# Latent keys and values of all batches made in the prologue, from chunk means that PE makes beside the transposes

## The chip, the cores and the metric

The kernel runs on one core of a Trainium2 chip. The metric is the device time of one execution in microseconds; of the kernel before there are three timed runs and one profiled execution. TensorE is called PE, VectorE DVE, ScalarE ACT, GpSimd POOL and SyncE SP, as in the profile; PEld is PE's loading of weights.

## What is computed

The input x has 4 batches of 1024 tokens with 256 features. It is normalised over the features to xn, and the output is x + attention(xn) + experts(xn).

- Attention is local, with 16 heads of 16 features over the last 128 tokens, and remote: the tokens of a batch are averaged in 64 chunks of 16 (`pooled`), `rkv = pooled @ rkv_w + rkv_b` gives latent keys and values (4 heads of 16 features each), and each token attends to the chunks before its own. A gate mixes both parts, and an output projection follows.
- The experts: a router picks 8 of 64 experts for each token, and their weighted outputs are added, with one shared expert for all tokens.

What matters here is that the latent keys and values of a batch depend on all its chunk means, while a block of 128 tokens uses only chunks that end before its tokens do. A batch has 8 blocks, and each block holds 8 chunks.

## The kernel before, in words

The 4096 tokens are 32 blocks (`NB`) of 128. Each engine has its own instruction stream, written out by hand, and semaphores tie them together.

**Prologue.** SP loads x in four parts, then the weights. DVE measures and normalises the blocks (`normalise`, L1204) into a ring of eight places (`xn_st`): a place is free again when PE has turned its block and SP has stored it to DRAM (L363, `xn_tiles`). PE goes through pairs of blocks (L660): `turn_x` transposes a pair into one of four PSUM banks (`turn_banks`, L648), and `route` of the pair before multiplies the transposed blocks with the router's weights (L656). ACT copies the transposed pair to `xT_all` (L935) and makes the router's scores (L939). Behind its last store SP fills the expert slots in DRAM with zeros (L368), 80 DMAs from the tile `zeros`, which is the second half of the experts' weight buffers. DVE then works out the routing: top groups (L1257 to L1279), top 8 (L1282, L1285), the selection (L1287), ranks with PE's help (L671, L673, then L1292 to L1301), slots (L1307 to L1335). POOL builds constants (L442 to L487), changes weights (L489 to L506), and adds the output bias to x (L513). When slots are known and the zeros have landed, it begins to scatter token rows to the experts' slots with indirect DMAs (L557). The order on PE is: turns and logits, rank products, attention.

**Attention** runs blocks 0 to 15 ahead of the experts and 16 to 31 behind them (`attention(start)`), the first two and the last of each half written out, 13 as a loop. A block's body has 8 steps `s`, one for each pair of heads, the same on PE, ACT and DVE. PE makes the scores of pair s (L741), turns the probabilities of pair s-2 (L755) and multiplies those of pair s-3 with the values (L767 to L769). DVE masks the scores and finds the maximum (L1457), ACT takes the exponential (L1033) and copies the turned probabilities (L1041). Projections of the next block, the shared expert and the remote part are spread over the steps. For the remote part of block i:

- ACT stages the transposed block in `xTs` (L976), DVE sums its 16-token chunks into `pooledT` and copies them a second time (`pool_chunks`, L1348 and L1350, at step 5 for the block after).
- PE's `latent_kv` (L771, step 3) waits for `pooled` and `remote_kept` and makes keys and values of the whole batch so far (L776, L778) in the bank `psM`; they count for chunks up to this block, and the mask `lat_wide` hides the rest.
- DVE's `keep_rkv` (step 3) adds the biases: L1407 spreads the keys over four heads (`rkz`), L1411 the values (`rv`).
- PE's `latent_scores` (L785, step 4), DVE's `latent_max` (L1421 to L1426, step 5), ACT's exponential (L1047), PE's turn and product (L791, L797, step 7), DVE's `latent_out`, and PE's projection one block later.

ACT's `keep_v_mid` (L988) copies the block's values for the windows that straddle two blocks; PE waits for it ahead of the values of pair 0 (step 3, L762). In the first half POOL scatters rows during attention, in the second it gathers the experts' rows (L609) and DVE adds them to x (L1506, twice a step). POOL's DMAs are paced by PE's steps (`pace`).

## Time and profile before

| | |
|---|---|
| timed runs | 1619.88, 1622.6, 1625.2 us; median 1622.6 |
| the profiled execution's own time | 1624.25 us |
| its span, first to last instruction | 1622.7 us |
| PE | 1340.4 us busy, 83% |
| weight loads on PE | 1235.2 us, 76% |
| DVE | 924.8 us, 57% |
| ACT | 905.3 us, 56% |
| POOL | 702.7 us, 43% |
| mean granted clock of PE | 0.91 |

Busy times are shares of the span. The shares are means over stretches that differ: prologue (to 131 us), first attention half, experts, second attention half. A float32 product of PE is two records in the trace, each with its own weight load; a transpose is one. Ends of matmuls are modelled. In a row the text in square brackets is the idle time of the engine before the instruction, and what ended it. "issue" stands for time without a wait that the profile shows.

### The profile page before, as it was taken

To read this page: it belongs to the slowest core of one execution; us is meant where nothing else is said; L and a number is where in the kernel's file an instruction comes from. 1 tells how busy PE (TensorE), PEld (TensorE's weight loads), DVE (VectorE), ACT (ScalarE), POOL (GpSimd) and SP (SyncE) were. 2 spreads that over 40 slices of the span, in tenths; PEclk is the share of its full clock that TensorE was granted. 3 is DMA by queue.
4 is the path that set the end of the run, shared out by engine and by line. 5 is a ranking of instruction groups with operands and counts; after the bars stand their busy time and mean duration, and the time that the engine had idled before them with its cause. 6 is when DMAs were issued, how large, how long until landed. Compare 5 with 4: busy or idle time off the path is not lost.

```text
span 1622.7 us, 38926 instructions
## 1 busy us (share of the span) xinstructions
PE 1340.4 (83%) x9257; PEld 1235.2 (76%) x9259; DVE 924.8 (57%) x3565; ACT 905.3 (56%) x2362; POOL 702.7 (43%) x841
## 2 busy tenths in 40 slices
PE   5117588788889889999999999999888888878885
PEld 4116478787788778988989898888777877778774
DVE  7986245555454553444444444434467777777775
ACT  2104355555555566666666666665545555555553
POOL 6601656656665621222222222100665656656550
PEclk9658689999898899999999999999898999989987
DMA  7999322222222215777777667654232223222220
GB/s 232 367 405 355 135 85 87 87 87 89 86 89 85 90 54 157 214 217 223 217 212 220 210 210 219 192 160 136 82 92 83 79 76 88 82 83 83 76 81 30
DMA packets 159339, 237.63 MB, mean 146 GB/s; under 512 B 21825, under 2 KB 127042, under 8 KB 159298
## 3 DMA queue, kind: packets, MB, share of 16 engines
q1 hardware_dynamic: 126658, 147.97, 27.4%
q0 software_dynamic: 32640, 89.17, 17.6%
q8 instruction: 18, 0.29, 0.1%
q14 instruction: 23, 0.19, 0.0%
HBM read 111.24 MB, written 125.83 MB: 146 GB/s over the span
## 4 chain that ended last, share of the span: by engine, by line
PE 66%; DVE 12%; issue 8%; another core or an unknown queue 7%; ACT 4%; SPq 1%; DVEq 1%; ACTq 0%; DMA 0%
PE psS L878 18%; PE psS L741 9%; PE psT L862 5%; PE psO L887 4%; PE psM L887 4%; PE psT L755 4%; PE psT L769 2%; PE psV L728 2%; PE psQ L688 2%; PE psV L699 2%; PE psQ L709 2%; DVE x_all L1506 1%; PE psO L767 1%; PE psO L769 1%
## 5 line engine op out<-in xcount | busy, mean ns | idle before, releaser
L609 POOL DMA_INDIRECT shared_mem<-slot_outs,idx_st x256 | 266.4, 1041 | 180.5 <-issue 64.0
L557 POOL DMA_INDIRECT slot_rows<-x_out_st,idx_st x256 | 257.7, 1007 | 165.0 <-issue 66.6
L878 PEld LDWEIGHTS psS<-sm,wt 128*128 128x128 f32 x2560 | 297.8, 191 | 40.4 <-ACT sm L1127 37.1
L878 PE MATMUL psS<-sm,wt 128*128 128x128 f32 x2560 | 323.9, 280 | 3.3 <-ACT sm L1127 1.9
L741 PE MATMUL psS<-kT,qz 128*128 128x192 f32 x1024 | 246.7, 368 | 29.6 <-DVE qz L1389 26.4
L1041 ACT COPY prT<-psT 128x384 f32<-128x384 f32 x256 | 122.0, 477 | 263.7 <-PE psT L755 135.3
L1142 ACT COPY wt<-shared_mem 128x512 f32 x320 | 197.8, 619 | 100.7 <-issue 98.4
L1033 ACT ACTIVATE pr<-sm,nmax 128x192 f32<-128x192 f32 x512 | 205.0, 449 | 59.9 <-DVE nmax L1457 47.9
L741 PEld LDWEIGHTS psS<-kT,qz 128*128 128x128 f32 x1024 | 182.4, 210 | 35.8 <-DVE qz L1389 26.9
L1457 DVE CUSTOM_DVE_ANT_0 sm<-psS,pr 128x192 f32<-128x192 f32 x512 | 162.3, 354 | 49.9 <-issue 48.2
L525 POOL DMA_DIRECT2D shared_mem<-in_L_ffn_We_gate x56 | 39.4, 704 | 334.2 <-PE psM L887 181.6
L1534 DVE TENSOR_TENSOR prT<-psS,prT 128x256 f32<-128x256 f32 x160 | 67.9, 425 | 201.1 <-ACT prT L1133 201.1
L755 PE MATMUL psT<-ident,pr 128*128 128x128 f32 x768 | 138.6, 293 | 30.6 <-ACT prT L1041 21.1
L755 PEld LDWEIGHTS psT<-ident,pr 128*128 128x128 f32 x768 | 106.6, 153 | 44.5 <-issue 36.2
L1506 DVE SCALAR_TENSOR_TENSOR x_all<-shared_mem,w,x_all (+1 forms) x256 | 123.5, 483 | 1.1
L1455 DVE MEMSET met<- 1x1 f32 x256 | 15.1, 59 | 179.4 <-PE psS L741 121.4
L1127 ACT COPY sm<-psT 128x512 f32<-128x512 f32 x160 | 93.6, 585 | 14.9 <-PE psT L862 8.5
L862 PE MATMUL psT<-ident,pr 128*128 128x128 f32 x640 | 96.5, 273 | 4.0 <-issue 3.1
L518 POOL COPY idx_st<-slot_idx 128x8 uint32 (+1 forms) x64 | 15.1, 238 | 188.3 <-DMA slot_outs<-sm 104.7
L1133 ACT ACTIVATE prT<-psS 128x256 f32<-128x256 f32 x160 | 61.3, 383 | 53.5 <-PE psS L878 48.5
L887 PE MATMUL psO<-shared_mem,prT 128*128 x320 | 82.5, 380 | 0.2 <-DVE prT L1534 0.2
L767 PE MATMUL psO<-v_mid,prT 128*128 128x72 f32 x256 | 49.5, 277 | 39.8 <-ACT v_mid L988 28.0
(255 smaller groups left out, 2630.1 us busy)
## 6 DMA issues: line engine op xcount, KB each, us to landing
slot_rows<-wt SPq DMA_DIRECT2D x80, 512.0 KB, 5.2
pr<-slot_rows SPq DMA_DIRECT2D x160, 256.0 KB, 3.1
slot_outs<-sm SPq DMA_DIRECT2D x160, 256.0 KB, 2.4
shared_mem<-in_L_ffn_We_gate POOLq DMA_DIRECT2D x56, 128.0 KB, 3.7
shared_mem<-in_L_ffn_We_up POOLq DMA_DIRECT2D x56, 128.0 KB, 3.9
shared_mem<-in_L_ffn_We_down POOLq DMA_DIRECT2D x56, 128.0 KB, 3.8
x_all<-in_L_attn_x SPq DMA_DIRECT2D x4, 1024.0 KB, 9.5
xn_tiles<-sm SPq DMA_DIRECT2D x32, 128.0 KB, 1.8
```

What stands on the lines that cost most here:

```text
L557: pool.indirect_dma_start(slot_rows, bass.IndirectOffsetOnAxis(ap=idx_st[:, j, k:k + 1], axis=0), x_out_st[:, j % 2, :], None).then_inc(sc ...
L609: pool.indirect_dma_start(rows_in[:, j, k, :], None, slot_outs, bass.IndirectOffsetOnAxis(ap=idx_st[:, j, k:k + 1], axis=0)).then_inc(rows ...
L741: last = mm(psS[:, p % 2, u * WIN:(u + 1) * WIN], qz[:, c, u, heads, :].rearrange("p h t -> p (h t)"), kT[:, c, u * UQ:u * UQ + WIN], star ...
L755: last = nc.tensor.transpose(psT[:, 0, a * P:(a + 1) * P], flat[:, a * P:(a + 1) * P], ident[:])
L862: last = nc.tensor.transpose(psT[:, j % 2, (a * DC + c) * P:(a * DC + c + 1) * P], xs[:, j, a, c * P:(c + 1) * P], ident[:])
L878: last = mm(psS[:, j % 2, (2 * a + n) * P:(2 * a + n + 1) * P], wt[j % 2][:, a, c, n * F:(n + 1) * F], xsT[:, j % 2, a, c, :], start=(c == ...
L887: last = mm((psM, psO)[j % 2][:, a * D:(a + 1) * D], hT[:, j % 2, a, :], ring_d[:, e % RING, :], start=True, stop=True)
L1033: nc.scalar.activation(pr[:, p % 4, par, :], sm[:, p % 4, par, :], ACT.Exp, bias=nmax[:, p % 4, par:par + 1], scale=-1.0).then_inc(probs, 1)
L1041: nc.scalar.copy(prT[:, p % 2].rearrange("p a t -> p (a t)"), psT[:, 0, 0:3 * P]).then_inc(prT_ready, 1)
L1142: last = nc.scalar.copy(wt[j % 2][:, a, :, :], ring_gu[:, e % RING, :, :])
L1457: v.tensor_tensor_reduce(sm[:, p % 4, u, :], psS[:, p % 2, u * WIN:(u + 1) * WIN], mask[:, u * WIN:(u + 1) * WIN], -1.0, -FLOOR, ALU.add, ...
L1506: ins = v.scalar_tensor_tensor(x_all[:, t, :], row, w8[:, t, k:k + 1], x_all[:, t, :], ALU.mult, ALU.add)
```

## The change

Latent keys and values are made once, in the prologue, for all four batches.

- POOL builds `chunk_of`, 128x8, with 1/16 where a token belongs to a chunk. In `turn_x` each transpose of PE is followed by a product with the same tile as weights and `chunk_of` as moving operand, which leaves the chunk means of the block in `psO`. The turns have three banks for it instead of four.
- ACT copies `psO` twice into `pooledT` behind the last scores; `pooledT` now lies in the first half of the experts' weight buffers. PE makes the keys of all batches (2 products of 256 columns) and the values (8 of 64 columns) in `psM`. ACT scales and biases the keys into `rkz`, in four instructions; DVE adds the biases of the values, in two, behind its top-8. PE's rank products wait for these.
- POOL prepares the key bias (`brkz`), and `consts` is raised behind it, after the weights have come.
- In attention `pool_chunks`, `latent_kv` and `keep_rkv` are gone, with their semaphores. `latent_scores` and `latent_values` pick their batch with `i // BPS`. `latent_scores` takes over the wait for `remote_kept`.
- Some tiles (`lsm`, `lneg`, `local`, `mixed`) move into `small`, for room. SP's order is as it was: the zero fill stands behind the last store of a normalised block.

The core of the diff:

```diff
-        pooledT = sb("pooledT", [P, DC, 2, NLAT])
-        rkz = sb("rkz", [P, LH, NLAT])
-        rv = sb("rv", [P, LH, LHD + 1])
+        chunk_of = sb("chunk_of", [P, LPB])
+        brkz = sb("brkz", [P, LH])
+        rkz = sb("rkz", [P, LH, B, NLAT])
+        rv = sb("rv", [P, B, LH, LHD + 1])
...
+        pooledT = wt[0][:].rearrange("p a c n -> p (a c n)").rearrange("p (c b a n) -> p c b a n", c=DC, b=B, a=2)
...
-        turn_banks = (psT[:, 0, :], psT[:, 1, :], psM[:], psO[:])
+        turn_banks = (psT[:, 0, :], psT[:, 1, :], psM[:])
...
+            after(nc.gpsimd.memset(chunk_of[:], 1.0 / CH))
+            fill(chunk_of[:], 0.0, [([[-CH, LPB]], 0, 1, ALU.is_ge), ([[CH, LPB]], CH - 1, -1, ALU.is_ge)])
+            pool.sem_inc(chunk_ready, 1)
...
-            nc.gpsimd.memset(pooledT[:], 0.0).then_inc(consts, 1)
             pool.wait_ge(w_in, W_ALL)
-            nc.gpsimd.tensor_scalar(brk[:], brk[:], float(CH), None, ALU.mult).then_inc(brk_ready, 1)
+            nc.gpsimd.tensor_tensor(brkz[:], rk_head[:], brk[:].broadcast_to([P, LH]), ALU.mult).then_inc(consts, 1)
...
-                if m >= 4:
-                    pe.wait_ge(xT_kept, m - 3)
+                if m >= 3:
+                    pe.wait_ge(xT_kept, m - 2)
                 for n in range(2):
                     for c in range(DC):
-                        last = nc.tensor.transpose(turn_banks[m % 4][:, (n * DC + c) * P:(n * DC + c + 1) * P],
-                                                   xn_st[:, (2 * m + n) % XN, c * P:(c + 1) * P], ident[:])
+                        part = xn_st[:, (2 * m + n) % XN, c * P:(c + 1) * P]
+                        nc.tensor.transpose(turn_banks[m % 3][:, (n * DC + c) * P:(n * DC + c + 1) * P], part, ident[:])
+                        at = c * B * NLAT + (2 * m + n) * LPB
+                        last = mm(psO[:, at:at + LPB], part, chunk_of[:], start=True, stop=True)
                 last.then_inc(xn_turned, 1)
...
+            pe.wait_ge(pooled, DC)
+            for c in range(DC):
+                mm(psM[:, 0:B * NLAT], wrkv[:, c, :], pooledT[:, c, :, 0, :], start=(c == 0), stop=(c == DC - 1))
+            for b in range(B):
+                at = B * NLAT + b * LD
+                for c in range(DC):
+                    last = mm(psM[:, at:at + LD], pooledT[:, c, b, :, :].rearrange("p a n -> p (a n)"), wrkv[:, c, LD:2 * LD],
+                              start=(c == 0), stop=(c == DC - 1))
+            last.then_inc(lat_kv, 1)
+            pe.wait_ge(rk_kept, LH + 2)
...
+            def batch(i):
+                return bass.ds(i // BPS, 1)
...
-            def latent_kv(i, nth):
-                pe.wait_ge(pooled, i + 1)
+            def latent_scores(i, nth):
+                pe.wait_ge(rq_kept, i + 1)
                 if nth:
                     pe.wait_ge(remote_kept, i)
-                for c in range(DC):
-                    mm(psM[:, 0:NLAT], wrkv[:, c, :], pooledT[:, c, 0, :], start=(c == 0), stop=(c == DC - 1))
-                for c in range(DC):
-                    last = mm(psM[:, NLAT:NLAT + LD], pooledT[:, c, :, :].rearrange("p a n -> p (a n)"), wrkv[:, c, LD:2 * LD],
-                              start=(c == 0), stop=(c == DC - 1))
-                last.then_inc(lat_kv, 1)
-
-            def latent_scores(i):
-                pe.wait_ge(rk_kept, 3 * i + 3)
-                pe.wait_ge(rq_kept, i + 1)
-                mm(psM[:, 0:LH * NLAT], rqT[:], rkz[:].rearrange("p h n -> p (h n)"), start=True, stop=True).then_inc(lat_s, 1)
+                mm(psM[:, 0:LH * NLAT], rqT[:], rkz[:, :, batch(i), :].rearrange("p h b n -> p h (b n)"), start=True, stop=True).then_inc(lat_s, 1)
...
-                              rv[:, 2 * n:2 * n + 2, :].rearrange("p h d -> p (h d)"), start=True, stop=True)
+                              rv[:, batch(i), 2 * n:2 * n + 2, :].rearrange("p b h d -> p (b h d)"), start=True, stop=True)
...
-                    if s == 3 and live:
-                        latent_kv(i, nth)
...
+            for a in range(2):
+                nc.scalar.copy(pooledT[:, :, :, a, :], psO[:].rearrange("p (c b n) -> p c b n", c=DC, b=B)).then_inc(pooled, 1)
+            act.wait_ge(lat_kv, 1)
+            act.wait_ge(consts, 1)
+            for h in range(LH):
+                nc.scalar.activation(rkz[:, h, :, :].rearrange("p b n -> p (b n)"), psM[:, 0:B * NLAT], ACT.Identity,
+                                     bias=brkz[:, h:h + 1], scale=rk_head[:, h:h + 1]).then_inc(rk_kept, 1)
...
-                    act.wait_ge(pooled, i)
...
+            dve.wait_ge(rk_kept, LH)
+            for par in range(2):
+                r = slice(par * NLAT, (par + 1) * NLAT)
+                tt(rv[r, :, par::2, 0:LHD],
+                   psM[r, B * NLAT:2 * B * NLAT].rearrange("p (b h d) -> p b h d", b=B, h=LH)[:, :, par::2, :],
+                   bcast(brv[r, :].rearrange("p (h d) -> p h d", h=LH)[:, par::2, :], B, 1), ALU.add).then_inc(rk_kept, 1)
...
-            def pool_chunks(i, blk, nth):
-                if nth:
-                    dve.wait_ge(lat_kv, i)
-                dve.wait_ge(xT_staged, i + 1)
-                src = xTs[:].rearrange("p c (n t) -> p c n t", t=CH)
-                v.tensor_reduce(pooledT[:, :, 0, bass.ds(blk * LPB, LPB)], src, AX_X, ALU.add).then_inc(pool_sums, 1)
-                dve.wait_ge(pool_sums, i + 1)
-                v.tensor_copy(pooledT[:, :, 1, :], pooledT[:, :, 0, :]).then_inc(pooled, 1)
...
-            def keep_rkv(i):
-                dve.wait_ge(lat_kv, i + 1)
-                v.scalar_tensor_tensor(rkz[:], bcast(psM[:, 0:NLAT], LH, 1), brk[:], bcast(rk_head[:], NLAT, 2),
-                                       ALU.add, ALU.mult).then_inc(rk_kept, 1)
-                for par in range(2):
-                    r = slice(par * NLAT, (par + 1) * NLAT)
-                    v.scalar_tensor_tensor(rv[r, par::2, 0:LHD],
-                                           psM[r, NLAT:NLAT + LD].rearrange("p (h d) -> p h d", h=LH)[:, par::2, :], 1.0 / CH,
-                                           brv[r, :].rearrange("p (h d) -> p h d", h=LH)[:, par::2, :],
-                                           ALU.mult, ALU.add).then_inc(rk_kept, 1)
...
-                        keep_rkv(i)
...
-                            pool_chunks(i + 1, next_blk, 1)
```

## Rows read from the trace of the kernel before

**Rows 1.** Busy time in stretches; columns: us, engines busy (records), PE clock, DMA share, GB/s.
```profile
22.00:32.00 10.00, 10.00 (x50) 9.96 (x49) 9.86 (x29) 2.54 (x5) 5.85 (x12) 1.00 0.65 218
33.00:48.00 15.00, 14.87 (x129) 14.07 (x129) 14.82 (x30) 8.79 (x15) 14.16 (x22) 1.00 0.46 161
...
620.00:1200.00 580.00, 562.26 (x4122) 509.29 (x4120) 267.00 (x988) 379.80 (x737) 154.36 (x217) 0.99 0.62 190
...
1320.00:1580.00 260.00, 216.60 (x1469) 202.65 (x1468) 192.29 (x756) 150.46 (x477) 154.29 (x162) 0.92 0.28 82
```

**Rows 2.** Chain of waits, prologue; columns: start us, us, what.
```profile
62.49 2.70 DVE shared_mem L1270
...
80.63 4.16 DVE top L1282 x32
...
131.26 2.93 PE psS L741 x8
```

**Rows 3.** PE's weight loads, then its last logits, from the timeline of the prologue.
```profile
20.25 1.57 PEld L648 LDWEIGHTS psT<-ident,sm 128*128 128x128 f32 x8 [3.23 <-issue]
...
28.50 0.87 PEld L648 LDWEIGHTS psT<-ident,sm 128*128 128x128 f32 x4
29.36 1.83 PEld L656 LDWEIGHTS psS<-gateT,xT_all 128*128 128x128 f32 x8
30.96 0.87 PEld L648 LDWEIGHTS psT<-ident,sm 128*128 128x128 f32 x4
...
37.40 0.97 PEld L656 LDWEIGHTS psQ<-gateT,xT_all 128*128 128x128 f32 x8
...
46.34 1.94 PE L656 MATMUL psV<-gateT,xT_all 128*128 128x64 f32 x16
```

**Rows 4.** Instructions grouped by line; columns: busy us, mean ns of one | idle before.
```profile
L776 PEld LDWEIGHTS psM<-pooledT,wrkv 128*128 128x128 f32 x128 | 16.8, 192 | 0.0
...
L1407 DVE SCALAR_TENSOR_TENSOR rkz<-psM,brk,rk_head 128x256 f32<-128x256 f32 x32 | 15.3, 480 | 39.6 <-remote 38.9 <-PE psM L778 0.6
...
L1348 DVE TENSOR_REDUCE pooledT<-xTs 128x256 f32 (+1 forms) x32 | 13.2, 412 | 0.0
...
L1411 DVE SCALAR_TENSOR_TENSOR rv<-psM,brv 64x32 f32<-64x32 f32 x64 | 11.8, 184 | 1.0
...
L1350 DVE COPY pooledT<-pooledT 128x128 f32<-128x128 f32 x32 | 7.3, 227 | 1.1
```

**Rows 5.** Timeline of PE in attention block 0.
```profile
135.68 0.82 PE L741 MATMUL psS<-kT,qz 128*128 128x192 f32 x4
```

**Rows 6.** Timeline of DVE in the routing, and POOL's bias additions.
```profile
50.44 1.53 DVE L1257 TENSOR_TENSOR shared_mem<-shared_mem 128x1024 f32<-128x1024 f32 x1
...
111.93 1.22 DVE L1301 TENSOR_TENSOR shared_mem<-sm 128x1024 f32<-128x1024 f32 x1
...
118.03 2.28 DVE L1329 TENSOR_TENSOR shared_mem<-shared_mem 128x2048 f32<-128x2048 f32 x1
...
39.70 28.79 POOL L513 TENSOR_TENSOR x_all<-x_all,bout 128x256 f32 x26
```

**Rows 7.** Timeline of SP's stores and of POOL's first step behind the zero fill.
```profile
22.91 23.23 SPq L363 DMA_DIRECT2D xn_tiles<-sm  x32
...
151.90 0.32 POOL L518 COPY idx_st<-slot_idx 128x8 uint32<-128x8 uint32 x2 [83.41 <-DMA slot_rows<-wt]
```

**Rows 8.** Waits; columns: us in total, times, longest us.
```profile
PE psO L767 <- ACT v_mid L988: 28.0, 24, 4.3
```

**Rows 9.** Chain of waits, attention: the removed instructions on it, first and last of each kind.
```profile
138.70 0.39 PE psM L776 x4
139.09 0.45 PE psM L778 x4
...
389.08 0.04 DVE rkz L1407
...
1186.69 0.42 DVE pooledT L1348
...
1527.04 0.39 PE psM L776 x4
...
1563.56 0.43 DVE pooledT L1348
...
1586.48 0.04 DVE rkz L1407
```

More of the change, by code:

```diff
@@ L153, in build @@
         prT = prT_mem[:, 0:6 * P].rearrange("p (j a t) -> p j a t", j=2, a=3)
-        lsm = sb("lsm", [P, LH, NLAT])
+        lsm, lneg = (small[:, n, :].rearrange("p (h n) -> p h n", h=LH) for n in range(2))
+        local, mixed = (small[:, n, :].rearrange("p (h d) -> p h d", h=H) for n in (2, 3))
         lmax = sb("lmax", [P, LH])
-        lneg = sb("lneg", [P, LH, NLAT])
         lpr = sb("lpr", [P, LH, NLAT])
@@ L461, in _ @@
             fill(own_head[:], 0.0, [([[-HD, HPC]], 0, 1, ALU.is_ge), ([[HD, HPC]], HD - 1, -1, ALU.is_ge)])
-            after(nc.gpsimd.memset(rk_head[:], LHD ** -0.5 / CH))
+            after(nc.gpsimd.memset(rk_head[:], LHD ** -0.5))
             fill(rk_head[:], 0.0, [([[-LHD, LH]], 0, 1, ALU.is_ge), ([[LHD, LH]], LHD - 1, -1, ALU.is_ge)])
@@ L483, in _ @@
             for par in range(2):
-                after(nc.gpsimd.memset(rv[par * NLAT:(par + 1) * NLAT, par::2, LHD:LHD + 1], 1.0))
+                after(nc.gpsimd.memset(rv[par * NLAT:(par + 1) * NLAT, :, par::2, LHD:LHD + 1], 1.0))
             after(nc.gpsimd.memset(lat[:], 0.0))
             after(nc.gpsimd.memset(lat[:, LD:LD + 1], 1.0))
-            nc.gpsimd.memset(pooledT[:], 0.0).then_inc(consts, 1)
             pool.wait_ge(w_in, W_ALL)
-            nc.gpsimd.tensor_scalar(brk[:], brk[:], float(CH), None, ALU.mult).then_inc(brk_ready, 1)
+            nc.gpsimd.tensor_tensor(brkz[:], rk_head[:], brk[:].broadcast_to([P, LH]), ALU.mult).then_inc(consts, 1)
             def gate_column(dst, src, g, n):
@@ L636, in _ @@
             pe.wait_ge(ident_ready, 1)
+            pe.wait_ge(chunk_ready, 1)
             for c in range(DC):
@@ L835, in body @@
                     if s == 4 and live:
-                        latent_scores(i)
+                        latent_scores(i, nth)
                     if s == 5 and live and ahead:
@@ L934, in keep_xT @@
                 act.wait_ge(xn_turned, m + 1)
-                nc.scalar.copy(xT_all[:, 2 * m:2 * m + 2, :, :].rearrange("p n c t -> p (n c t)"), turn_banks[m % 4]).then_inc(xT_kept, 1)
+                nc.scalar.copy(xT_all[:, 2 * m:2 * m + 2, :, :].rearrange("p n c t -> p (n c t)"), turn_banks[m % 3]).then_inc(xT_kept, 1)
             def keep_scores(n):
@@ L1046, in latent_exp @@
                     act.wait_ge(lat_turned, i)
-                nc.scalar.activation(lpr[:], lneg[:], ACT.Exp, scale=-1.0).then_inc(lat_p, 1)
+                nc.scalar.activation(lpr[:], lneg, ACT.Exp, scale=-1.0).then_inc(lat_p, 1)
             def keep_lprT(i):
@@ L1459, in mask_pair, with body @@
                                            nmax[:, p % 4, u:u + 1]).then_inc(masked, 1)
-            def body(i, blk, nth, live=True, tail=True, ahead=True, last_tail=True, next_blk=None, combining=False):
+            def body(i, blk, nth, live=True, tail=True, ahead=True, last_tail=True, combining=False):
                 if live:
@@ L1483, in body @@
                         latent_max(i, blk)
-                        if ahead:
-                            pool_chunks(i + 1, next_blk, 1)
                     if s == 6 and tail:
```

26 lines of the change are left out of this document (11 added, 15 removed).

## The prediction

> **What bounds the kernel now.** I read the table by stages first [rows 1]. The kernel has four stretches: a prologue up to the first scores at 131 us, attention over the first 16 blocks, the experts, attention over the other 16. From 620 to 1200 us PE is busy 562 of 580 us and the change touches nothing there. In attention PE is the busiest engine (217 of 260 us in the second stretch) and is never full; DVE follows with 192, because the expert rows are added there.
>
> Then the chain of waits of the prologue [rows 2]. It stays on DVE, which works through the routing (62.49 and 80.63 are steps of it) almost without a pause, until the first scores at 131.26. So whatever makes DVE begin the routing later moves everything behind it, one for one.
>
> What sets that begin is in the timeline of PE and DVE [rows 3]. PE takes turns: 4 transposes, then 8 records of router logits (a float32 product is two records), for each pair of blocks. Eight weight loads of the logits take 1.83 us at 29.36 and 0.97 at 37.40: PE is at its lower clock (1.2 GHz) first and at 2.4 GHz later. The clock column says 1.00 over both stretches, the durations do not, and I go by them: 50 records in 10.00 us against 129 in 15.00 [rows 1]. At the lower level a pair takes 2.46 us (28.50 to 30.96) with PE busy throughout; at the higher one 12 records take 12 x 15.00 / 129 = 1.40. The last logits end at 46.34 + 1.94 = 48.28.
>
> **The change, part by part.**
>
> *Chunk sums on PE.* Each transpose gets a product beside it, the same tile as weights against an 8-column matrix: 4 a pair, 8 records, 128 in all. The trace has no product of 8 columns. The nearest are the logits of 64 columns: 8 records between the loads at 29.36 and 30.96, 1.60 us at the lower level, and 0.97 at the higher [rows 3]. Each record loads 128x128 float32 weights, and a load takes 192 ns for 64 columns too [rows 4], so I don't expect fewer columns to shorten the step. Bound below: nothing, if such a product hid under its transpose; above: the logits' price. I take the latter, because the loads stand end to end already.
>
> The Trainium skill has a rule that would make it cheap: by "TensorE: Matmul & The Clock Gate", section "Wait — 56ns, not 53.3ns?", starts can be about 25 ns apart when a product is narrow. By that the 128 records would cost 3.2 us and the kernel would end near 1614 us, as an estimate from that page. The rows speak against it here, since the loads alone are 0.11 to 0.20 us apart.
>
> *Which clock.* PE rose to the higher level only after some twelve us of gapless transposes and 64-column logits (20.25 to about 32 us), while in the first attention block, behind 192-column scores, eight records take 2.93 us at 131.26 and four take 0.82 at 135.68 [rows 2, 5]. So a rise comes soon behind wide products and late behind narrow ones, and the change thins the narrow stream further, with 8 of 20 records only 8 columns wide. I take PE at 1.2 GHz through the whole stage. A pair costs 2.46 + 1.60 = 4.06 us, 16 of them 65.0, from 20.25 to 85.2: **36.9 us later** than 48.28.
>
> *What DVE gets back.* POOL adds the output bias to the blocks (L513) until 68.5 us [rows 6], and DVE is slower beside it: 128x1024 elements take 1.53 us at 50.44 but 1.22 at 111.93; 128x2048 take 2.70 at 62.49 [rows 2] against 2.28 at 118.03 [rows 6]. With blocks staged more slowly POOL is done before DVE's routing begins (DVE stages eight blocks ahead, so the last is staged when PE has turned 12 pairs, 20.25 + 12 x 4.06 = 69; PE ends at 85). DVE's steps from 50.44 to 70.67 then cost: two of 1024 at 1.22, four of 512 at 0.69, five of 256 at 0.42 (both by the line through 1.22 and 2.28), three of 2048 at 2.28, with 0.4 of gaps: 14.6 instead of 20.2. With 0.5 on the last step of 512 ahead of them that gives back **6.1 us**.
>
> *Small things in the prologue.* Two additions for the values on DVE, about 0.23 each by the copy of L1350, against the first chunk reduction and copy (0.41 + 0.23 [rows 4]), which leave the same path: zero. The 20 PE records for keys and values (about 5 us at the lower level), and six ACT steps of at most 0.6 us each, lie under the 29 us that DVE then takes from its first routing step to the end of the top-8 (80.63 + 4.16 - 50.44 now [rows 2, 6], less 5.6). If DVE were quicker there, its wait for the keys would show. POOL's chunk matrix (three short steps, half a microsecond) comes near 3 us, long before PE turns at 20.25. Three turn banks instead of four: ACT has two pairs' time, 8 us, for a copy. No DMA is added. The zero fill starts behind the last block's store (46.14 now) and so some 24 us later; it ends near 176 instead of 151.9 [rows 7], 14 us after the new first scores instead of 21, so POOL's scatter isn't later relative to attention. The first passes through new code in attention are slower than the later ones; with the code's new place that could move, and I leave 4 us either way for it.
>
> **Prologue: +36.9 - 6.1 = +30.8 us.**
>
> *Attention.* For each block PE loses 8 records (0.88 us at the higher level), DVE five instructions: 0.48 + 2 x 0.18 + 0.41 + 0.23 = 1.49 us [rows 4]. Over 32 blocks that is 28 and 48 us; the end sees little of it. Right behind the removed PE products, PE waits for ACT's v_mid copy, 24 times, 28.0 us in all [rows 8]. That copy hangs on the turn of pair 1, ahead of the products removed, so PE arrives 0.9 us earlier and waits 0.9 us longer. Where PE has no such wait the products stand on the chain, in blocks 0, 1, 15 and 29: 4 x 0.84 = 3.4 us [rows 9]. DVE's pooling steps stand on the chain ten times in the second half (1186.69 the first, 1563.56 the last), each 0.9 us with its gaps; the key and value steps seven times over both halves, 0.5 us each [rows 9]. That is 3.4 + 9 + 3.5 = 16 us. The next in line is close, with PE and DVE both near full there, so I take **-12 us**, bounds 0 and -35 (all of PE's share). PE now picks a batch by register, a few 0.1 us on its sequencer, which I cost at nothing: the sequencer runs ahead where it can use its wait for v_mid, and would cost up to 0.2 us a block without that cover.
>
> **Sum.** 1624.25 + 30.8 - 12 = 1643.0 for the profiled execution, which is 1.65 us above the median of the three runs; against the median 1641.4. I say **1641**.
>
> **Rivals.**
> 1. *PE rises to 2.4 GHz in the prologue after all* (this is the one that isn't slower). If at 32.3 us as now: 3.0 pairs by then, 13 at 1.40 + 0.97 = 2.37 us, end at 63.1, +14.8 - 6.1 = +8.7, total **1619**. If behind the first pair: 15 at 2.37, end at 59.9, about 1616. For it: nothing in PE's stream is idle. Against: the late rise now. It decides from a rise before about 45 us. The Trainium skill is on its side: on the same page, section "What's actually happening", the default state is throttled and activity releases it; the trace has 12 us of gapless activity before the release. By that rule at its quickest the total would be the 1616. Chance 0.14.
> 2. *The loops are bound by PE's records alone*: all 8 count in each block, 32 x 1.1 us = -35 instead of -12, total **1618**. For it: PE is the busiest engine. Against: the waits right behind. Chance 0.09.
> 3. *The longer idle time in front of v_mid drops PE's clock more often*: it already stands at 0.92 over the loops of the second half [rows 1]. Each low stretch costs at least the 2.46 - 1.40 = 1.1 us that a pair of the prologue costs more, say 1.7; ten more of them +17, and the gain of 12 gone: **1670**; half of it 1656. Chance 0.09.
> 4. *My own case*, 0.68.
>
> **How the numbers follow.** About 0.3% (4.9 us) is what a measurement of this kernel can tell from no change. Of rivals 1 and 2 about half ends below 1617.7: faster 0.11; most of the rest within 0.3%: same 0.12; slower 0.77. My case alone spans 1622.6 + 27 - 25 = 1625 to 1622.6 + 35 - 0 = 1658; rivals 1 and 2 stretch the low end to 1618, half of rival 3 the high end to 1658.
>
> **What would show it.** Loads of L648 at 0.87 us for four up to the last pair, last logits at 85 us, DVE's 128x1024 routing steps at 1.22 us each, first scores at 162, experts ending some 25 us later than now. The wait of L767 for v_mid near 2 us a block. Loads at 0.42 before 45 us would be rival 1; a block period down by over 1 us rival 2; a granted clock below 0.90 over the loops rival 3.

## The result, and the profile after

The kernel after took 1631.62 us (median of 9 runs, 1623.71 to 1634.98), the kernel before 1622.6 in the same session (9 runs, 1616.19 to 1628.23). The ratio is 1.0042, 95% interval 1.0022 to 1.0063: **slower by 0.4%**, 7 to 9 us. The forecast was slower by 18. The profiled execution took 1631.97 us, its span is 1630.4 and its mean granted clock 0.926; the span is 7.7 us longer than that of before. The ratios are worked out over all rounds of runs and are not quotients of the medians beside them; where all runs count the two differ by up to 0.3% (the medians of e9 alone would give 0.985, its ratio is 0.9876). Runs over 1.5% slower than the fastest of their kernel count as slow and stay out of its ratio: there are four of 12 in e3 and one of six in e11, whose medians are of all runs.

The groups of work of the page of after, of the whole span:

```profile
PE 1364.0 (84%) x9149; PEld 1252.0 (77%) x9151; DVE 871.8 (53%) x3407; ACT 906.0 (56%) x2368; POOL 693.9 (43%) x843
...
L1453 DVE MEMSET met<- 1x1 f32 x256 | 15.1, 59 | 232.0 <-PE psS L758 169.3
...
L784 PE MATMUL psO<-v_mid,prT 128*128 128x72 f32 x256 | 53.7, 297 | 72.9 <-ACT v_mid L1000 53.1
```

DVE has 53 us less to do than before (871.8 against 924.8), near the 48 of the forecast's count. Its wait for the scores grew (121.4 us before, 169.3 now) and PE's wait for `v_mid` nearly doubled, from the 28.0 us of [rows 8] to 53.1 in 24 blocks: what left both engines became idle time in good part.

**The prologue.** The stretches that answer to [rows 1], in the table of busy time by stretch of after:

```profile
core 0: us, PE busy (x) PEld busy (x) DVE busy (x) ACT busy (x) POOL busy (x), PEclk, DMA share, GB/s
22.00:32.00 10.00, 10.00 (x55) 10.00 (x55) 8.41 (x24) 1.76 (x3) 5.48 (x11) 1.00 0.61 198
33.00:48.00 15.00, 15.00 (x80) 15.00 (x80) 10.89 (x24) 2.50 (x5) 14.16 (x23) 1.00 0.21 71
48.00:82.00 34.00, 34.00 (x178) 34.00 (x177) 6.71 (x14) 8.35 (x14) 10.16 (x15) 1.00 0.60 229
```

The columns are us, then the busy time of each engine with its records, PE's granted clock, the DMA share and GB/s. PE is busy without a gap and does 80 records in the 15 us in which it did 129 before; it doesn't get faster later. The weight loads show at which level, as in [rows 3]:

```profile
28.87 1.83 PEld L660 LDWEIGHTS psS<-gateT,xT_all 128*128 128x128 f32 x8
30.46 0.34 PEld L651 LDWEIGHTS psT<-ident,sm 128*128 128x128 f32 x1
30.68 0.55 PEld L653 LDWEIGHTS psO<-chunk_of,sm 128*128 128x128 f32 x2
...
32.71 0.55 PEld L660 LDWEIGHTS psS<-gateT,xT_all 128*128 128x128 f32 x2
```

Eight loads take 1.83 us, the lower level, here and in the last pairs (1.83 at 74.95). A pair takes 32.71 - 28.87 = 3.84 us. The chain of waits then gives the milestones that answer to [rows 2]:

```profile
79.00 3.52 PE psV L660 x16
82.55 0.61 ACT shared_mem L944
...
84.00 1.24 DVE shared_mem L1269
...
158.07 1.23 DVE qz L1398
159.34 2.93 PE psS L758 x8
```

Last logits at 82.52, first scores at 159.34 instead of 131.26: **28.1 us later**. The end is only 7.7 later, so 20.4 came back behind the first scores. All these are of one profiled execution of each kernel.

**Where they came back.** DVE copies a mask at the start of each block; its rows mark the blocks. Before:

```profile
131.12 0.35 DVE L1358 COPY pr<-masks 128x384 f32<-128x384 f32 x1
150.72 0.35 DVE L1358 COPY pr<-masks 128x384 f32<-128x384 f32 x1
199.42 0.36 DVE L1358 COPY pr<-masks 128x384 f32 x1 [0.23 <-issue]
...
575.42 0.36 DVE L1358 COPY pr<-masks 128x384 f32<-128x384 f32 x1
```

After:

```profile
159.21 0.35 DVE L1367 COPY pr<-masks 128x384 f32<-128x384 f32 x1
188.32 0.35 DVE L1367 COPY pr<-masks 128x384 f32<-128x384 f32 x1
220.14 0.36 DVE L1367 COPY pr<-masks 128x384 f32 x1 [0.23 <-issue]
...
596.42 0.36 DVE L1367 COPY pr<-masks 128x384 f32<-128x384 f32 x1
```

Blocks 0 and 1 took 199.42 - 131.12 = 68.3 us before and 60.9 after: **7.4 us back at once**. Blocks 2 to 14 take 376.0 and 376.3, nothing gained. The rest, 13.0 us, comes behind block 15's start, nearly all in the second half. That first piece was not in the forecast. POOL's first scatter shows what differs there. In before it is prepared at 151.90 [rows 7], 20.6 us behind the first scores; in after:

```profile
171.04 0.32 POOL L519 COPY idx_st<-slot_idx 128x8 uint32<-128x8 uint32 x2 [105.35 <-DMA slot_rows<-wt]
```

that is 11.7 us behind them, because the fill hangs on the stores and moved by 19 us, less than the scores.

### The profile page after: what moved, and what is told of

It is laid out like the page before. It is cut to its first block, busy times and chain, and to the rows that moved or that the text cites. A ratio compares the mean times of both kernels' runs of the same rounds, so it can differ in the third digit from the quotient of the medians.

```text
span 1630.4 us, 38498 instructions
## 1 busy us (share of the span) xinstructions
PE 1364.0 (84%) x9149; PEld 1252.0 (77%) x9151; DVE 871.8 (53%) x3407; ACT 906.0 (56%) x2368; POOL 693.9 (43%) x843
## 4 chain that ended last, share of the span: by engine, by line
PE 71%; DVE 11%; issue 9%; another core or an unknown queue 4%; ACT 3%; DMA 1%; DVEq 0%; SPq 0%; ACTq 0%
PE psS L883 18%; PE psS L758 9%; PE psT L867 4%; PE psT L772 4%; PE psO L892 4%; PE psM L892 4%; PE psQ L705 3%; PE psV L716 2%; PE psV L745 2%; PE psT L786 2%; DVE x_all L1501 2%; PE psQ L726 2%; PE psO L784 2%; PE psO L786 1%
## 5 line engine op out<-in xcount | busy, mean ns | idle before, releaser
L758 PE MATMUL psS<-kT,qz 128*128 128x192 f32 x1024 | 253.3, 376 | 28.3 <-DVE qz L1398 26.2
L758 PEld LDWEIGHTS psS<-kT,qz 128*128 128x128 f32 x1024 | 188.6, 216 | 37.1 <-DVE qz L1398 26.6
L1453 DVE MEMSET met<- 1x1 f32 x256 | 15.1, 59 | 232.0 <-PE psS L758 169.3
L784 PE MATMUL psO<-v_mid,prT 128*128 128x72 f32 x256 | 53.7, 297 | 72.9 <-ACT v_mid L1000 53.1
L784 PEld LDWEIGHTS psO<-v_mid,prT 128*128 128x128 f32 x256 | 46.4, 227 | 80.3 <-issue 70.3
L519 POOL COPY idx_st<-slot_idx 128x8 uint32 (+1 forms) x64 | 15.7, 247 | 210.3 <-DMA slot_rows<-wt 105.4
```

The lines of the kernel that those rows point to most:

```text
L758: last = mm(psS[:, p % 2, u * WIN:(u + 1) * WIN], qz[:, c, u, heads, :].rearrange("p h t -> p (h t)"), kT[:, c, u * UQ:u * UQ + WIN], star ...
L784: mm(dst, prT[:, p % 2, 1, :], v_mid[:, p, :], start=True, stop=False)
```

## The experiments

All ran in later sessions, where the kernel before had medians of 1610 to 1613 us; each ratio is against before on the same chip. The table puts together what the mask rows of each profiled execution give, in us: start of block 0, length of blocks 0 and 1 together, mean period of blocks 2 to 14, time from block 15's start to block 16's (it holds the experts), mean period of blocks 18 to 30. The rows of before and after are of the first session, where before was some 10 us slower than later, and part of that lies in the periods: e1 has the loops of before, and its periods are 28.3 and 28.8. So the periods of the experiments are to be compared with each other.

```text
kernel                  block 0  0 and 1  2 to 14  15->16  18 to 30  ratio to before
before                   131.1    68.3     28.9    558.7    29.2     1
after                    159.2    60.9     28.9    558.4    28.2     1.0042
e1 before+products       158.5    60.4     28.3    562.6    28.8     1.0121
e2 after-products        130.7    68.0     28.7    561.8    28.0     0.9938
e3 64 columns            158.9    58.7     28.8    560.2    27.6     0.9972
e4 sums on DVE           136.3    65.8     28.6    558.0    27.5     0.9941
e5 before, paced         132.0    50.4     28.7    566.4    28.4     0.9952
e6 after, PE back        158.1    63.6     28.6    557.2    27.9     1.0038
e7 after, DVE back       158.2    61.3     28.3    557.5    27.9     1.0090
e8 after, warm-up        158.9    61.4     28.4    560.1    27.3     1.0026
e9 e4, paced             136.1    45.8     28.4    567.6    27.5     0.9876
e10 PE back 3 times      158.4    61.0     28.7    565.0    28.3     1.0120
e11 DVE back 3 times     158.3    59.7     29.0    559.6    28.5     1.0151
e12 128 columns          134.6    68.2     28.6    558.1    27.8     0.9951
e13 after, paced         158.4    45.0     28.5    567.0    27.5     0.9996
e14 e12, paced           134.0    49.1     28.6    567.2    27.7     0.9884
e15 both back            158.3    61.3     28.3    558.8    28.3     1.0102
e16 e9, last unpaced     138.0    45.0     30.0    558.5    27.4     0.9917
```

### The two parts of the change, each alone

e1 is the kernel before with the products and the three banks that they need, and nothing else of the change:

```diff
+    nc.tensor.transpose(turn_banks[m % 3][...], part, ident[:])
+    last = mm(psO[:, at:at + LPB], part, chunk_of[:], start=True, stop=True)
```

> The kernel before, with the 8-column products beside the transposes and three turn banks, their results used by nobody; the loops are those of before. Theory A (the prologue costs what the trace of after shows, PE at 1.2 GHz throughout, and the loops are unaffected by it): first scores at 131.3 + 28 = 159.5 us, and the end 28 us later too, 1650 us. Theory B (a later start of the loops against POOL's zero fill shortens the first two blocks by 7.4 us, 68.3 to 60.9 between before and after): first scores at 159.5, but the end only some 21 us later, 1643, with the second block under 35 us long instead of 48.7. Theory C (my forecast's sizes: pair 4.06 us): first scores at 162, end at 1653.

1632.58 us against 1611.06, ratio **1.0121** (1.0086 to 1.0157), +19.5 us. First scores at 158.60, and blocks 0 and 1 take 60.4 us with the old loops. So the 7.4 us belong to the later start, not to the removed work: theory B, whose +21 us was also the nearest.

e2 is the complement, the kernel after without the products. It leaves out the chunk means; ACT copies other values in their place:

```diff
-    last = mm(psO[:, at:at + LPB], part, chunk_of[:], start=True, stop=True)
...
-    nc.scalar.copy(pooledT[:, :, :, a, :], psO[:]...)
+    nc.scalar.copy(pooledT[:, :, :, a, :], xT_all[:, 0:2, :, :]...)
```

> The kernel after without its 8-column products: the latents are computed from the first two blocks' values, so the sums are left out; everything else stands. Theory A: the products are the whole cost of the prologue, first scores at 131 to 132 us, and the loops give back 20 us as in the trace of after: 1602. If the 7.4 us of the first two blocks come from the later start alone (theory B), they are not given back here: 1610. If the forecast's 12 us for the loops were right: 1611, with the rest of what was given back between before and after being the later start.

1600.57 us, ratio **0.9938** (0.9916 to 0.996), -10 us. Scores start at 130.79 as before, and blocks 0 and 1 take 68.0 us although the work is gone from them. The loops alone bring 10 us, close to the 12 of the forecast and to theory B; the 20 of theory A are out. The two ratios multiply to 1.0058, inside the interval of after: the parts add up.

### What the first two blocks wait for

POOL's scatters are paced by attention: ahead of some of them it waits for a count of pairs that PE has turned or multiplied. If they start late, that count has long been reached, and POOL issues them without a break until it has caught up. e5 moves the counts of the first half by six pairs:

```diff
-    pace(at, g * (SCATTER_HALVES // 2), isinstance(g, int) and g == 0)
+    pace(at, g * (SCATTER_HALVES // 2) + 6, isinstance(g, int) and g == 0)
```

> The kernel before, with POOL's scatters of the first half paced six score pairs later against attention, so that they don't start with a backlog. Theory B1 (the first two blocks take 68 us where POOL's scatters start 20 us behind the first scores, and 59 to 61 where they start 12 us behind, because POOL then issues 21 to 25 indirect DMAs with no break, 1.27 us apart, and holds PE's semaphore updates meanwhile; with the late start it is 16): the first unbroken run of scatters is 16 or fewer, the first two blocks take 58 to 62 us instead of 68, and the end comes about 7 us earlier, ratio 0.996. Rival B2 (the long second block is the first pass through new code, whatever POOL does): first two blocks 66 to 69 us, ratio 1.00.

1603.14 us, ratio **0.9952** (0.9931 to 0.9973). Blocks 0 and 1 take 50.4 us, far less than expected. The first unbroken run of scatters has 10 DMAs instead of 23. The idle time of PE from 154 to 184 us, in the table of its lines, first before, then e5 (the last column is the idle time ahead):

```profile
L785 PE MATMUL psM<-rkz,rqT 128*128 128x256 f32 x2 | 1.2, 715 | 8.0 <-issue 8.0
L767 PE MATMUL psO<-v_mid,prT 128*128 128x72 f32 x4 | 1.2, 408 | 4.2 <-issue 4.2
```

```profile
L767 PE MATMUL psO<-v_mid,prT 128*128 128x72 f32 x8 | 2.1, 359 | 2.7 <-issue 2.7
```

In before a third such stop runs out of that stretch: 9.29 us, up to 188.72. DVE and ACT stand there too: ACT's next copy of turned probabilities has 22.46 us of idle time ahead of it.

But of the 18 us gained there 8 are lost again: from block 15 to 16 it takes 566.4 us instead of 558.7. The last scatter is as early as before, yet now it starts 24.8 us behind block 15's start (580.4 - 555.6) instead of 5.2, and the experts need all of them.

e13 does the same to the kernel after.

> The kernel after with the pacing of e5. Theory B1 (the late start already took most of the scatters' backlog away, 60.9 us for the first two blocks): first two blocks 57 to 61 us, ratio to before 1.002 to 1.005, where the same pacing took 0.5% off the kernel before. Rival (the pacing gains everywhere, by spreading the scatters over the whole half): ratio to before 0.999 or less.

1611.95 us, ratio **0.9996** (0.9973 to 1.0019). That is 0.46% less than after, as much as the pacing brought to before; the theory's numbers were missed. Blocks 0 and 1 fell from 60.9 to 45.0 us. The late start had taken away a third of the backlog's cost, not all of it: 7 of some 20 us. The rival asked for 0.999 or less, which the interval doesn't exclude, but its reason doesn't hold: blocks 2 to 14 take 28.5 us each, as in e8 (28.4) and e3 (28.8), the same loops unpaced.

e9 paces e4 (below), and e16 is e9 with the last of its eight groups unpaced:

```diff
-    pace(at, g * (SCATTER_HALVES // 2) + 6, ...)
+    pace(at, g * (SCATTER_HALVES // 2) + (0 if isinstance(g, int) and g else 6), ...)
```

> The kernel of e9, but the last of the eight groups of scatters is paced as before, without the lag. If the experts' stretch was 8 us longer in e9 because its last scatters ended 23 us behind the last block's start instead of 5: they end 5 to 15 us behind it now, and the end comes 3 to 8 us earlier than in e9, ratio to before 0.983 to 0.986. If the stretch grew for another cause: 0.987 to 0.989 as in e9.

1598.48 us, ratio **0.9917** (0.9893 to 0.9941): worse than e9's 0.9876, against the expectation. The experts' stretch did go back, to 558.5. But where POOL catches up its six pairs, in block 14, the hold of the first blocks appears again. The mask rows of e16:

```profile
497.23 0.36 DVE L1365 COPY pr<-masks 128x384 f32 x1 [0.38 <-issue]
525.58 0.36 DVE L1365 COPY pr<-masks 128x384 f32 x1 [0.38 <-issue]
573.27 0.36 DVE L1365 COPY pr<-masks 128x384 f32<-128x384 f32 x1 [0.32 <-issue]
```

Its POOL, the first and the last of 20 DMAs about 1.27 us apart, and the one behind them:

```profile
532.84 0.96 POOL L554 DMA_INDIRECT slot_rows<-x_out_st,idx_st  x1 [0.30 <-PE psT L779]
534.11 0.97 POOL L554 DMA_INDIRECT slot_rows<-x_out_st,idx_st  x1 [0.31 <-DMA slot_rows<-x_out_st,idx_st]
...
557.04 0.96 POOL L554 DMA_INDIRECT slot_rows<-x_out_st,idx_st  x1 [0.30 <-issue]
560.39 0.96 POOL L554 DMA_INDIRECT slot_rows<-x_out_st,idx_st  x1 [2.40 <-remote]
```

And its PE and ACT. PE stands for 15.41 us and goes on 2.2 us behind the end of POOL's run (558.00):

```profile
540.92 0.81 PE L765 MATMUL psT<-ident,pr 128*128 128x128 f32 x3
...
559.62 0.48 ACT L1048 COPY prT<-psT 128x384 f32<-128x384 f32 x1 [18.87 <-remote]
...
560.24 0.88 PE L765 MATMUL psT<-ident,pr 128*128 128x128 f32 x3 [15.41 <-issue]
```

The block takes 47.7 us; in before it was block 1 that took 48.7. So neither the first pass through the code nor the zero fill makes that block long. It is long wherever POOL works off a backlog of indirect DMAs. What ACT's copy at 559.62 waits for, the turn of 540.92 and products ahead of it, was done by 541.73 (ends on PE are modelled), 17.9 us earlier. So the work was ready and its release came late. How POOL's run does that no row shows: the profile puts PE's wait down to nothing ("issue") and ACT's to "remote".

### The clock in the prologue

e3 and e12 widen the chunk matrix with zero columns; each product overwrites what the one before spilled, so the means stay the same.

```diff
-    last = mm(psO[:, at:at + LPB], part, chunk_of[:], start=True, stop=True)
+    wide = min(P, (c + 1) * B * NLAT - at)
+    last = mm(psO[:, at:at + wide], part, chunk_of[:, 0:wide], start=True, stop=True)
```

> The kernel after with a chunk matrix of 64 columns instead of 8 (56 of them zero; later products overwrite their columns, so the sums are the same). Theory A (a record costs its weight load and PE stays at 1.2 GHz behind any narrow stream): pair 3.84 us or up to 0.2 us more, end within 0 to +4 us of after, 1632 to 1636. Rival (what keeps PE at 1.2 GHz is the narrowness of the products): the weight loads of the logits fall from about 1.8 us for eight to 0.97 at some point before 60 us, and the kernel ends 10 to 20 us earlier than after, 1612 to 1622.

64 columns: 1615.96 us, ratio 0.9972 (0.9934 to 1.001), no clear difference from before. The profiled execution took 1623.12 us and stays at the lower level: pair 3.84 us, to the hundredth that of 8 columns. So by the profile it is theory A, by the ratio the rival. The times are in two groups, five from 1597 to 1605 and seven from 1616 to 1624. A rise in some executions would explain them, and the mean granted clock parts them too: 0.905 to 0.911 in the first, 0.915 to 0.927 in the second, beside 0.899 to 0.912 in e12, which rose, and 0.915 to 0.932 in after. No profile of the first group was taken, so that is not shown.

> The kernel of e3 with a chunk matrix of 128 columns instead of 64. e3's times fell into two groups, 1597 to 1605 (five of 12) and 1616 to 1624 (seven), and the profiled one, of the upper group, had PE at 1.2 GHz throughout the turn stage. Theory W (wider products make PE rise to 2.4 GHz in more executions, which then end some 20 us earlier): 9 or more of 12 in a lower group around 1600. Rival V (the width does not matter; the two groups come from elsewhere): the same share as e3, or all near 1620 to 1630, since a record of 128 columns is at least as long as one of 64.

128 columns: 1601.79 us, ratio **0.9951** (0.9927 to 0.9974), all 12 runs below 1610. The timeline of PE in e12:

```profile
22.64 0.42 PE L651 MATMUL psT<-ident,sm 128*128 128x128 f32 x1
22.85 0.63 PE L654 MATMUL psO<-chunk_of,sm 128*128 128x128 f32 x2
...
23.88 0.27 PE L651 MATMUL psT<-ident,sm 128*128 128x128 f32 x1
23.99 0.39 PE L654 MATMUL psO<-chunk_of,sm 128*128 128x128 f32 x2
24.88 1.00 PE L661 MATMUL psS<-gateT,xT_all 128*128 128x64 f32 x8
...
27.05 1.00 PE L661 MATMUL psS<-gateT,xT_all 128*128 128x64 f32 x8
```

PE rises to 2.4 GHz 3 us behind its first transpose (20.69), ahead of the first logits. A pair takes 2.17 us instead of 3.84, and the first scores come at 134.75. Sixteen times the columns made the product cheaper, by the clock alone: ahead of the rise a transpose and its product took 0.64 us instead of 0.53. The edit narrows the last products again, to 8 columns for block 31, and PE keeps the higher level there:

```profile
50.38 0.97 PEld L661 LDWEIGHTS psV<-gateT,xT_all 128*128 128x128 f32 x8
...
52.42 0.97 PEld L661 LDWEIGHTS psV<-gateT,xT_all 128*128 128x128 f32 x8
```

The Trainium skill ("TensorE: Matmul & The Clock Gate", section "What's actually happening") says that the default state is throttled and that activity releases it. e12 agrees. After differs: its PE is busy without a gap from 20.83 to 82.52 and stays at 1.2 GHz, and there the measurement decides.

e8 tries to have the clock before the stage, by six products of 512 columns on zeros:

```diff
+    for n in range(6):
+        mm(psV[:], ident[:], zeros[:, 0:512], start=True, stop=True)
     pe.wait_ge(gate_in, 32)
```

> The kernel after with six products of 512 columns (zeros, used by nobody) on PE in the idle stretch from about 4 us on, ahead of the gate's transposes. Theory C1 (PE rises to 2.4 GHz behind wide products and keeps it while the turn stage gives it no gap): eight loads of the logits take 0.97 us from the first pair on, pairs 2.3 us, first scores 20 us or more earlier than in after, at 133 to 140 us; the end 10 to 20 us earlier, ratio to before 0.992 to 0.998. Rival C2 (the level falls back, in the idle time before 20 us or behind the narrow products): pairs 3.84 us as in after, ratio to before 1.004.

```profile
4.27 8.27 PE L639 MATMUL psV<-wt,ident 128*128 128x512 f32 x12 [4.27 <-POOL wt L453]
16.94 0.47 PE L643 MATMUL psM<-ident,dif 64*128 64x64 f32 x2 [4.40 <-DMA gbias<-in_L_ffn_gate_bias]
20.48 0.45 PE L654 MATMUL psT<-ident,sm 128*128 128x128 f32 x1 [3.07 <-DVE sm L1219]
```

1617.56 us, ratio 1.0026 (1.0001 to 1.0051): within the interval of after, rival C2. The clock did rise: of the 12 records the first start some 0.85 us apart, those from 10.24 on 0.43. But behind the idle time of 4.40 us the gate's transposes take 0.47 us, as in after without the warm-up, the transposes behind 3.07 more take 0.45, the lower level, and the pairs 3.84 again.

### What the loops gained, and on which engine

e6 puts the 8 PE records of a block back into after, e10 three times; e7 the five DVE steps, e11 three times; e15 one set of each. All work on constants, and nobody uses the results.

```diff
     if s == 3 and live:
+        products_back(i, nth)
...
     keep_v(i, 1, nth)
+    steps_back(i)
...
     latent_max(i, blk)
+    sums_back(i)
```

> The kernel after with the 8 PE records a block that it removed put back in their old place, on constant operands and used by nobody. Theory D (what the loops gained, they gained on DVE, in the second half, where DVE also adds the expert rows; PE's records stood ahead of a wait for v_mid): mean block period of the second half 28.5 us as in after, ratio to after 1.000 to 1.002. Rival P (PE's records are the gain): period 29.2, ratio to after 1.007, that is 1.011 to before.

> The kernel after with the five DVE steps a block that it removed put back in their old places, on constant operands and used by nobody (one copy reads from SBUF where the old one read PSUM). Theory D (the gain of the loops is DVE's): mean block period of the second half 29.2 us as in before, against 28.5 in after; ratio to before 1.010. Rival P: period 28.5, ratio to before 1.004.

e6: 1615.96 us, ratio **1.0038** (1.0009 to 1.0066), that of after. PE's wait for `v_mid` falls from 53.1 to 25.2 us: the products go back into the hole that they left. e7: 1624.39 us, **1.0090** (1.0056 to 1.0124), 0.5% above after. e8, after with a warm-up that changed nothing, ran in the same session and took 1617.56: e6 is 1.6 us below it, e7 6.8 above. The block periods don't bear that out. The expectations count them over blocks 16 to 30 (29.2 in before, 28.5 in after), and so counted e6 has 28.2, e7 28.3 where 29.2 was expected, and e8 27.7.

There is a second reason why e6 costs nothing, and the forecast had it as its rival 3. A record of the scores takes 326 ns at the higher level and 527 at the lower. Over blocks 2 to 14 the share of records over 500 ns is 8.7 to 11.8% in the six kernels that have the PE products (before, e1, e5, e6, e10, e15) and 12.6 to 20.0% in the other twelve; over blocks 16 to 30 it is 5.4% in e6 and 16.4% in e8. With the products gone PE is at the lower level more often, and with them put back it isn't. So that e6 costs nothing doesn't show that the products were free: they fill a wait, and they keep the clock up. The runs don't part the two.

> The kernel after with the 8 removed PE records a block put back three times (24 records, used by nobody). Theory D (the first 8 fit into the wait for v_mid, 53.1 us over 24 blocks in after, 2.2 us each; a set costs 0.88 us): the first two sets are nearly free and the third costs up to 0.5 us a block: ratio to before 1.004 to 1.013. Rival P (each PE record counts): 24 x 0.11 = 2.6 us a block, +84 us in all less what the slow first blocks hide: ratio 1.04 or more.

> The kernel after with the five removed DVE steps a block put back three times. Theory D (DVE's steps stand on the path for about a third to a half of their 1.5 us a block in e7, +8 us for one set): three sets cost at least three times that, 24 us or more, since what slack there is goes to the first: ratio to before 1.019 or more, and the second half's period over 30 us. Rival (DVE has slack and e7's +8 us were an accident of the measurement): ratio under 1.012.

e10: 1625.56 us, 1.0120 (1.0076 to 1.0164), at the upper end of theory D and far from the 1.04 of the rival; the wait for `v_mid` is used up, 4.0 us. e11: 1638.37 us, 1.0151 (1.0107 to 1.0196), less than three times one set; its interval just reaches the expected bound, and the period in the second half is 28.5 to 28.8 us, not the 30 expected.

> The kernel after with both the 8 PE records and the five DVE steps a block put back, on constants, used by nobody, so without the old waits of one engine for the other (sums to products, products to keys and values, these to the scores). If the work is the gain: ratio to before 1.011 to 1.013, as for the kernel before's loops behind the same prologue (e1, 1.0121), mean period of the last 13 intervals 28.5 us or more. If the hand-over between PE and DVE is a part: ratio 1.006 to 1.010 (the sum of e6 and e7), period 28.0 to 28.3.

e15: 1628.41 us, **1.0102** (1.0065 to 1.0140), between the two ranges, with an interval that covers both; the period is 28.3, the top of the second. Against e1 (1.0121), the same prologue with the real old loops, 0.2% is left for the old waits between PE and DVE, which the intervals don't tell from nothing.

### Versions that beat both

e4 drops the products and lets DVE make the chunk sums behind its selection step, where it waits for PE's ranks; keys and values follow behind the ranks.

```diff
     tt(sel_b[:], ra_t, rb_t, ALU.not_equal).then_inc(sel_ready, 1)
+    for c in range(DC):
+        v.tensor_reduce(x_out_st[:, c, :], xT_all[:, :, c, :]..., AX_X, ALU.add).then_inc(chunks_summed, 1)
```

> The kernel after without the products; instead DVE makes the chunk sums in two reductions of 4096 elements a partition (8.6 us at the 0.41 us for 256 less 0.1 fixed... by the row of the old reduction, 1.05 ns an element) behind its selection step, where it waits 3.8 us for PE's ranks; the latents follow behind the ranks. Theory A (each us on DVE's path in the prologue moves the end by one, the loops give back what they gave in after): first scores at 131.3 + 8.6 - 3.8 = 136 us, end at 1602 + 5 = 1607. Rival: DVE's relief from POOL's additions is gone with the fast turn stage, and the loops' gain hangs on the late start: 1615 or more.

```profile
93.71 8.74 DVE L1296 TENSOR_REDUCE x_out_st<-xT_all 128x256 f32<-128x4096 f32 x2
102.37 0.68 DVE L1302 COPY shared_mem<-psQ 128x512 f32<-128x512 f32 x1
```

1601.66 us, ratio **0.9941** (0.9915 to 0.9968). The sums take 8.74 us, of which the wait for the ranks hides 3.5; first scores at 136.47, 5.2 later than before. The end was forecast worse than the start: 9.4 us gained against the median of before, where theory A had 15.6 (1607 against 1622.6) and the rival at most 7.6. Theory A took over the 20 us of the loops, of which e2 left 10. Blocks 0 and 1 are long again (65.8 us). So it was paced too:

> The kernel of e4 (chunk sums on DVE behind its selection step) with the pacing of e5 (scatters six score pairs later). If the two gains are of different places, as I hold: first scores at 136, first two blocks 58 to 61 us, ratio to before 0.9941 x 0.9952 = 0.989, about 1593 us where before has 1610. Rival: both come from the same hold, since e4's first two blocks were 66 us, two less than before: ratio 0.992 to 0.995.

e9: 1586.54 us, ratio **0.9876** (0.9833 to 0.9919), the lowest of all and as the two gains added up; blocks 0 and 1 took 45.8 us, less than the 58 to 61 expected. And the change's own scheme, with wide products and pacing:

> The kernel of e12 (chunk matrix of 128 columns) with the pacing of e5. Theory B1: first scores at 135, first two blocks 58 to 61 us instead of 68, ratio to before 0.9951 - 0.0045 = 0.988 to 0.992. Rival: no gain over e12, ratio 0.994 to 0.997.

e14: 1593.74 us, ratio **0.9884** (0.9846 to 0.9923), with blocks 0 and 1 at 49.1 us. The intervals of e9 and e14 overlap, so which of them is the faster stays open.

## Why the prediction was right or wrong

The direction, the range and the prologue were right, the size was not: +18 us where 7 to 9 were measured. The sum for the profiled execution was +30.8 - 12 = +18.8; its span grew by 7.7. Step by step:

- **Which clock: right.** Eight loads take 1.83 us up to the last pair; rival 1 did not happen. e12 shows that it was a matter of the products and not of idle time on PE: with 128 columns it rose after 3 us. The forecast weighed a rise "behind wide products" only as an argument for its own case and never asked what wider products would do.
- **Chunk sums on PE: right in kind, a little too dear.** A pair costs 3.84 us, not 4.06: the eight records add 1.38, not 1.60, so 0.17 us each, not 0.20. The stage ends at 82.5 instead of 85.2. The 25 ns between starts of narrow products that the Trainium skill gives ("TensorE: Matmul & The Clock Gate", section "Wait — 56ns, not 53.3ns?") was 7 times too little as a cost here; the weight loads set the pace, as the rows had said, since 64 columns cost no more than 8 (e3, 3.84 us a pair).
- **What DVE gets back: right.** From the last logits to the first scores it took 131.26 - 48.28 = 83.0 us before and 159.34 - 82.52 = 76.8 after: 6.2 back, forecast 6.1. DVE's 128x1024 steps take 1.22 to 1.24 us. Prologue in all: +28.1 for +30.8.
- **Attention -12: right for the removed work.** Beyond blocks 0 and 1 the trace gives 13.0, e2 gives 10. The wait for `v_mid` was forecast at 2 us a block and is 53.1 / 24 = 2.2. That DVE's steps and not PE's records are the gain is what the times of e6 and e7 point to; how it is shared out stays open, since three sets cost less than three times one and the block periods don't follow. The forecast had 3.4 of its 16 us on PE's products, for which e6 shows no net cost. Rival 2 is out: PE's records put back cost nothing, where it asked for 35 us. Rival 3 is out at its price but right in kind. The granted clock of the second half went from 0.92 [rows 1] to 0.91 (1330 to 1590 us), and the share of score records over 500 ns from 13.0 to 15.7% over blocks 16 to 30; their mean went from 368 to 374 ns.
- **The step that failed: "The zero fill ..., so POOL's scatter isn't later relative to attention"**, which priced the place of the scatters at zero, with "4 us either way" for the first passes through new code. I had worked out that they would start 14 us behind the first scores instead of 21 (measured 11.7 and 20.6), and had asked only whether that could do harm. It does good. A scatter that starts earlier relative to attention has a smaller backlog, POOL's unbroken run falls from 23 DMAs to 16, and blocks 0 and 1 take 7.4 us less. e1 shows this with the old loops (60.4 us), e2 its absence with the new ones (68.0); e5, e13 and e16 move the backlog and the hold moves with it. The long block 1 was in the trace of before, 48.7 us beside blocks of 29, and I took it for new code. Why a run of scatters holds the other engines stays open.

The account: prologue 2.7 us less than forecast, first two blocks 7.4 less, the other blocks 1.0 less. That makes the 11.1 by which 18.8 missed 7.7. Most of what the products cost in the prologue was real; part of it was paid back by a cost that before had and nobody had looked for.

## What to carry to other kernels

When a change delays one stream against another, ask for each producer that is paced by the other how large its backlog is at the start, before and after; a block that is much longer than its neighbours is worth an explanation before the forecast. A product that is bound by its weight load can be made wider at no cost (up to 64 columns here), and where PE sits at its lower clock behind narrow products it is worth trying. Work that leaves an engine right ahead of a wait is worth nothing until the wait is gone; here eight records a block could leave and come back unseen, and without them PE was at its lower clock more often.

## What was not expected of the hardware

- PE stayed at 1.2 GHz through 62 us of unbroken work (20.83 to 82.52) of transposes, 8-column and 64-column products, and rose 3 us after the start of the same stage with 128-column products. Once up, it stayed up while the products narrowed to 8 columns. The column of the granted clock said 1.00 in both; only the durations tell them apart.
- Six products of 512 columns raised the clock 6 us in, for nothing: behind an idle time of 4.40 us PE was at the lower level again.
- A run of 20 indirect DMAs of POOL, one each 1.27 us, goes with stops of PE of up to 15.41 us and of ACT of up to 22.46, in whichever block it falls (block 1 in before, e2, e4 and e12, block 14 in e16). POOL's DMAs spread out over the half cost little of this: blocks 0 and 1 take 45 to 50 us when paced, 59 to 68 otherwise.
